# A recurrent sandwich block on one Trainium2 core: rounding GpSimd's weight pieces by two adding transfers instead of two elementwise instructions

## What is computed

```python
def layer_1(x, W_in, b_in, W_out, b_out, gamma, beta):
    u = einsum('bsd,hd->bsh', x, W_in) + b_in
    def step(state, u_t):
        s = tanh(u_t + state * gamma + beta)
        return (s, s)
    states = scan(step, 0, u)
    return einsum('bsh,dh->bsd', states, W_out) + b_out

def quantized_matmul(x, w, scale):
    wq = w.astype(float8_e4m3fn).astype(x.dtype)
    return einsum('bsi,io->bso', x, wq) * scale

def layer_2(x, gate_w, up_w, down_w, gate_scale, up_scale, down_scale):
    gate = silu(quantized_matmul(x, gate_w, gate_scale))
    up = quantized_matmul(x, up_w, up_scale)
    return quantized_matmul(gate * up, down_w, down_scale)

x = x + layernorm(layer_1(layernorm(x), ...))
x = x + layernorm(layer_2(layernorm(x), ...))
```

## Time and profile before

| | |
|---|---|
| runs (median of 3) | 603.26 us (601.48 to 605.08) |
| the profiled execution | 603.18 us, its span 601.4 us |
| TensorE busy (PE) | 557.9 us, 93% |
| VectorE busy (DVE) | 398.2 us, 66% |
| ScalarE busy (ACT) | 325.5 us, 54% |
| GpSimd busy (POOL) | 208.7 us, 35% |
| chain that ended last | DVE 35%, PE 32%, ACT 21%, issue 5%, DMA 4% |
| transfers | 27.47 MB, all issued by SyncE |

### The profile page before, as it was taken

The page is one execution under the profiler, slowest core; times in us unless marked ns, Lnnn a source line. Parts: engine busy times, 40 slices in busy tenths (PEclk is TensorE's granted clock), DMA queues, the critical chain, the costliest instruction groups (busy, mean ns, idle before and its releaser), DMA issues.

```text
span 601.4 us, 10100 instructions
## 1 busy us (share of the span) xinstructions
PE 557.9 (93%) x2984; PEld 467.4 (78%) x2984; DVE 398.2 (66%) x1638; ACT 325.5 (54%) x1496; POOL 208.7 (35%) x335
## 2 busy tenths in 40 slices
PE   4999798899899999999999999999999997988993
PEld 4766465789779887988788988988798786876992
DVE  3987967778686666766685758665666677655213
ACT  2765564655557554755466545755575555551330
POOL 1100214356637232534244314432233233521622
PEclk9999899899999999999999999999999998999998
DMA  8774114001012001010012001200010000200000
GB/s 267 212 243 143 53 44 150 1 19 36 1 36 71 1 1 36 14 58 2 1 36 71 1 1 36 71 2 1 1 41 32 1 1 2 71 1 1 37 0 35
DMA packets 16598, 27.47 MB, mean 46 GB/s; under 512 B 2336, under 2 KB 4512, under 8 KB 16544
## 3 DMA queue, kind: packets, MB, share of 16 engines
q1 hardware_dynamic: 16544, 26.84, 13.9%
HBM read 22.63 MB, written 4.19 MB: 45 GB/s over the span
## 4 chain that ended last, share of the span: by engine, by line
DVE 35%; PE 32%; ACT 21%; issue 5%; DMA 4%; POOL 1%; SPq 1%; POOLq 0%; DVEq 0%; ACTq 0%
DVE recur L934 17%; ACT pairs L1215 12%; PE gate_up L854 11%; PE wide L811 6%; DVE fused L1050 5%; PE wide L880 4%; ACT pairs L1202 4%; PE wide L789 4%; ACT gated L1238 3%; PE wide L765 3%; ACT fused_hi L1254 2%; PE wide L898 1%; DVE x_norm L1024 1%; DVE z L1062 1%; DVE y L974 1%
## 5 line engine op out<-in xcount | busy, mean ns | idle before, releaser
L934 DVE TENSOR_TENSOR_SCAN recur<-recur,pairs 128x32 f32<-128x32 f32 x1024 | 235.7, 230 | 139.8 <-ACT pairs L1215 139.5
L1215 ACT ACTIVATE pairs<-recur 128x16 f32<-128x16 f32 x1024 | 191.8, 187 | 211.3 <-DVE recur L934 206.6
L811 PE MATMUL wide<-w_out_sb,pairs 128*128 128x512 f32 x256 | 116.0, 607 | 10.0 <-ACT pairs L1215 9.8
L1325 POOL TENSOR_TENSOR fused_lo<-fused,fused_hi 128x256 fp32r<-128x256 f32 x96 | 72.0, 750 | 145.6 <-ACT fused_hi L1254 145.5
L811 PEld LDWEIGHTS wide<-w_out_sb,pairs 128*128 128x128 f32 x256 | 74.7, 298 | 44.4 <-ACT pairs L1215 9.5
L789 PE MATMUL wide<-x_norm_t,w_in_sb 128*128 128x256 f32 x448 | 102.7, 386 | 6.3 <-ACT x_norm_t L1170 3.2
L854 PE MATMUL gate_up<-x_hi,gate_q 128*128 128x256 f32 x384 | 103.3, 301 | 4.4 <-DVE x_lo L1035 4.4
L789 PEld LDWEIGHTS wide<-x_norm_t,w_in_sb 128*128 128x128 f32 x448 | 85.1, 193 | 21.8 <-ACT x_norm_t L1170 6.3
L854 PE MATMUL gate_up<-x_lo,up_q 128*128 128x256 f32 x384 | 97.3, 286 | 0.0
L854 PE MATMUL gate_up<-x_hi,up_q 128*128 128x256 f32 x384 | 96.9, 285 | 0.0
L854 PE MATMUL gate_up<-x_lo,gate_q 128*128 128x256 f32 x384 | 96.5, 284 | 0.0
(11 more groups left out here) (93 smaller groups left out, 563.7 us busy)
## 6 DMA issues: line engine op xcount, KB each, us to landing
x_in<-x SPq DMA_DIRECT2D x16, 256.0 KB, 3.2
x_res<-x SPq DMA_DIRECT2D x16, 256.0 KB, 3.3
out<-z SPq DMA_DIRECT2D x14, 256.0 KB, 3.6
w_in_sb<-w_in_t SPq DMA_DIRECT2D x4, 512.0 KB, 5.6
w_out_sb<-w_out_t SPq DMA_DIRECT2D x8, 256.0 KB, 5.1
raw_own<-gate_w SPq DMA_DIRECT2D x6, 256.0 KB, 5.9
raw_own<-up_w SPq DMA_DIRECT2D x6, 256.0 KB, 4.2
z<-down_w SPq DMA_DIRECT2D x6, 256.0 KB, 3.0
```

The lines of the kernel that those rows point to most:

```text
L811: ins = eng.matmul(wide[b][:, :], pairs_by_batch[:, state_slots(n, b), :, j, 0].rearrange("p s b -> p (s b)"), w_out_sb[:, j, :], start=(j ...
L934: eng.tensor_tensor_scan(preact.rearrange("p c k -> p (c k)"), factors.rearrange("p c k -> p (c k)"), pairs[:, (t - 1) % RING, :, :].rearr ...
L1215: eng.activation(pairs[:, t % RING, :, 0], preact[:, :, 1], ACT.Tanh).then_inc(s_state, 1)
L1325: eng.tensor_tensor(fused_lo[:, f, :], fused[:, f, :], fused_hi[:, f, :].bitcast(F32), ALU.subtract).then_inc(s_fused_lo, 1)
```

## The change

For each of GpSimd's ten pieces the two elementwise instructions are replaced by three: GpSimd writes the negated constants into the piece's place in `down_q` (counted by a new semaphore), issues a transfer that adds the constants to the raw piece where it lies, and, when that has landed and the negation is done, issues a second transfer that adds the raw piece to the negated constants in `down_q`. Every wait on `s_pool_taken` counts 16 for a piece now, since a transfer raises its semaphore by 16. One line is added further up, so lines from 565 on stand one later. The timetable's costs are not changed.

```diff
--- before.py
+++ after.py
@@ -562,6 +562,7 @@
         s_constant = sem("s_constant")
         s_rounded = sem("s_rounded")
         s_taken = sem("s_taken")
+        s_pool_negated = sem("s_pool_negated")
         s_pool_rounded = sem("s_pool_rounded")
         s_pool_taken = sem("s_pool_taken")
         s_guard_step = sem("s_guard_step")
@@ -673,7 +674,7 @@
                     if before is not None:
                         eng.wait_ge(s_peak, 2 * (before + 1))
                         if by_pool(before):
-                            eng.wait_ge(s_pool_taken, pool_pieces(before + 1))
+                            eng.wait_ge(s_pool_taken, 16 * pool_pieces(before + 1))
                         else:
                             eng.wait_ge(s_rounded, tensor_pieces(before + 1))
                     eng.dma_start(raw[r], pieces[i][0]).then_inc(s_raw_in[r], 16)
@@ -698,7 +699,7 @@
                 yield T * n + 40.0
                 if n == 1:
 
-                    eng.wait_ge(s_pool_taken, pool_pieces(EARLY))
+                    eng.wait_ge(s_pool_taken, 16 * pool_pieces(EARLY))
                     eng.wait_ge(s_rounded, tensor_pieces(EARLY))
                     eng.wait_ge(s_peak, 2 * EARLY)
                 if n >= 2:
@@ -840,7 +841,7 @@
                             eng.wait_ge(s_x1_lo, batch * (p + 1))
                         if p == 0 and i % 4 == 0:
                             eng.wait_ge(s_taken, 2 * tensor_pieces(8 * (i // 4 + 1)))
-                            eng.wait_ge(s_pool_taken, pool_pieces(8 * (i // 4 + 1)))
+                            eng.wait_ge(s_pool_taken, 16 * pool_pieces(8 * (i // 4 + 1)))
                         if i < batch and p < LAST - 1:
 
                             eng.wait_ge(s_x_norm_t, batch * (p + 2) + i + 1)
@@ -864,7 +865,7 @@
                         eng.wait_ge(s_fused_lo, KI * p + i + 1)
                         if p == 0:
                             if by_pool(GATE_UP_PIECES + i):
-                                eng.wait_ge(s_pool_taken, pool_pieces(GATE_UP_PIECES + i + 1))
+                                eng.wait_ge(s_pool_taken, 16 * pool_pieces(GATE_UP_PIECES + i + 1))
                             else:
                                 eng.wait_ge(s_taken, 2 * tensor_pieces(GATE_UP_PIECES + i + 1))
                             if i == KI - 1:
@@ -1130,7 +1131,7 @@
                 eng.tensor_scalar(guard[:, 2:3], guard[:, 1:2], HUGE, HUGE, ALU.mult, ALU.mult).then_inc(s_guard_step, 1)
                 yield at["guard", 3]
                 eng.wait_ge(s_guard_step, 3)
-                eng.wait_ge(s_pool_taken, pool_pieces(NP))
+                eng.wait_ge(s_pool_taken, 16 * pool_pieces(NP))
                 eng.scalar_tensor_tensor(out=poisoned, in0=guard[:, 2:3], scalar=0.0, in1=poisoned.bitcast(F32),
                                          op0=ALU.mult, op1=ALU.add).then_inc(s_guard_step, 1)
 
@@ -1332,11 +1333,13 @@
                     src, constant = raw[raw_of[i]], rounders[:, i % NR, :].bitcast(F32)
                     yield at["pool_add", i]
                     eng.wait_ge(s_constant, i + 1)
+                    eng.tensor_scalar(pieces[i][1], constant, -1.0, 0.0, ALU.mult, ALU.add).then_inc(s_pool_negated, 1)
                     eng.wait_ge(s_peak, 2 * (i + 1))
-                    eng.tensor_tensor(src, src, constant, ALU.add).then_inc(s_pool_rounded, 1)
+                    eng.dma_start(src, constant, accum_op=ALU.add).then_inc(s_pool_rounded, 16)
                     yield at["pool_take", i]
-                    eng.wait_ge(s_pool_rounded, pool_pieces(i + 1))
-                    eng.tensor_tensor(pieces[i][1], src, constant, ALU.subtract).then_inc(s_pool_taken, 1)
+                    eng.wait_ge(s_pool_negated, pool_pieces(i + 1))
+                    eng.wait_ge(s_pool_rounded, 16 * pool_pieces(i + 1))
+                    eng.dma_start(pieces[i][1], src, accum_op=ALU.add).then_inc(s_pool_taken, 16)
 
             strands = [prepare(), low_parts(), round_weights()]
             for b in range(batch):
```

## The result

The changed kernel takes 619.5 us (median of 4 runs, 618.01 to 621.14), the kernel before 602.37 us beside it (4 runs): ratio 1.028, 95% interval 1.023 to 1.033. The forecast was 616.8 us, with a range of 606 to 637. The span grew from 601.4 to 617.9 us, by 16.5.

A forecast was written before the change was run, and what follows sets the result against it. The recurrence on VectorE was taken to end last in the edited stretch, with TensorE nearly full behind it. Waits of 1.3 + 6.9 + 5.9 - 0.5 = 13.6 us on 603.18 us gave 616.8 us, range 606 to 637.

The forecast's parts named there:

- first place: Pieces 26 and 27: piece 32's reload lands late, so VectorE's maxima at 106.33 come 1.3 us late.
- Second place: Pieces 29 to 31: piece 35's reload makes VectorE's maxima at 140.98 6.9 us late; the y root's wait hides in it.
- Third place: Pieces 34 and 35: the last guard step on VectorE, at 171.10, waits for the last landing, 5.9 us late.
- The gain: VectorE's exponent mask at 120.23, lengthened by GpSimd's add, stands beside the shorter negation instead: minus 0.5 us.
- D and L: D: GpSimd's time to issue a transfer, taken as 1.0 us; L: start of issue to landing, taken as 3.7 us.
- S: 3L + D, the sum in which both transfer prices enter at all three places: 12.1 us.
- VectorE blocks the issue: Rival: each issue waits 0.43 us for a VectorE mask or constants instruction on the shared port; 620.7 us, chance 0.11.
- the projection's own wait would grow past 2.12 us: Sign: TensorE's wait before the output projection at 160.68 grows past its earlier 2.12 us.
- TensorE waits a little for low part 4: Second place: low part 4 is queued behind the y root, but TensorE waits less than VectorE is late.
- GpSimd's busy time would fall by 18 us: Sign: GpSimd's busy time falls by about 18 us while the kernel's time rises.
- Two bounds of its rivals: Not slower: S under 5.7, 602.1 to 602.7 us, chance 0.04; nearly hidden: L 2.0 to 2.2, 603.2 to 606.3, 0.11.
- general form: max(0, S - 10.8) + max(0, S - 5.2) + max(0, S - 6.2) - 0.5, as growth for any S.

The follow-up runs named there:

- e5: Changed kernel with the timetable told the transfers' times, so each second issue stands later with other work between and VectorE's readers are placed by landings: 602.0 us, ratio 1.0002.
- e3: Changed kernel with the maxima of pieces 31 to 35 left out: 614.9 us, ratio 1.020.
- e6: Changed kernel with the last guard step on VectorE six steps of the recurrence later: 617.5 us, ratio 1.025.
- e7: As e3, with the y root moved ahead of piece 31 on GpSimd: 616.3 us, ratio 1.022.
- e1: Changed kernel keeping each piece's first transfer, with an elementwise subtraction for the second and no negation: 613.4 us, ratio 1.018.
- e9: Changed kernel plus one adding transfer of 1 KB issued by GpSimd at 83.16 us: 617.5 us, ratio 1.025.
- e4: Changed kernel plus one adding transfer of 1 KB issued by GpSimd at 8.29 us: 617.9 us, ratio 1.027.
- e2: Changed kernel with an elementwise add for the first transfer, keeping negation and second transfer, whose landing is awaited piece by piece: 610.0 us, ratio 1.013.
- e10: Changed kernel with the loads of pieces 29 and 30 cut to 8 of 512 columns: 621.3 us, ratio 1.031.
- e11: As e5, with pieces 24 and 25 also GpSimd's, twelve pieces in place of ten: 605.1 us, ratio 1.006.
- e12: Changed kernel with the loads of x for the third block and of pieces 29 and 30 cut to 8 of 512 columns: 619.2 us, ratio 1.029.

## Why the prediction held

**The mechanism.** GpSimd in order behind landings, VectorE in order behind GpSimd: shown by e5, which has the same instructions, the same bytes and the same engines, with GpSimd's and VectorE's programs in another order, and none of the loss; and by the waits named in e3, e6 and e7. Forecast of the changed kernel, 616.8 us; measured, 619.5. Growth forecast 13.6 us; span's growth 16.5. By scans the terms miss by +1.6 us (first place), +1.3 (the constants of piece 32, not in the sum), -1.8 (second), -1.2 (third), -0.2 (gain) and +3.3 (what the sum lacked). That the total is nearer than that is partly luck, since the misses have both signs.

**D and L.** Taken as 1.0 and 3.7 us. Measured: issues of 1.09 and 0.87 us in the mean for the pieces in raw_own, landings of 3.6 and 3.2. At the second place piece 29's first issue starts at 134.01 and piece 30's second at 143.06, which lands 3.2 us later, at 146.3. Of these 12.3 us piece 30's negation takes 0.57 (138.38 to 138.95), so S is 11.7 us, against 12.1. The Trainium skill, DMA: Bandwidth & Descriptors ("Anatomy of one DMA"), led to an estimate of L = 2.6 us and 608.9 us for the kernel; these transfers landed in 3.2 to 3.6, so the rows of the trace were the better guide.

**First place: +1.3 forecast, +2.9 measured.** The failing step is one L for all transfers: piece 26's first one landed in 6.0 us, and piece 27 was taken at 106.3, not at 104.8. It also makes the reload of piece 31 late (1.87 us), which the prediction passed over for that of piece 32 (0.82 us).

**Second place: +6.9 forecast; +5.1, and +1.3 just before it at the constants of piece 32, measured.** The constants reuse piece 28's, so they wait for its second landing, 0.66 us: a wait on VectorE that I had not listed. The other half is that they take 0.94 us beside low part 2, in place of 0.42. Piece 35's reload lands when it does, so what VectorE lost here it doesn't lose again there. The sum, 6.4, is within 0.5 of the forecast by a term that the forecast did not have. That the root hides behind the reload was right (e3); that the residual hides behind the root I did not see (e7).

**Third place: +5.9 forecast, +4.7 measured.** Piece 35 landed 13.1 us behind the end of low part 11, not 13.7: the negation takes 0.57 us before the issue starts, not 0.8, twice. And low part 11 came 9.4 us late, when the recurrence was 9.8 late already.

**The gain: -0.5 forecast, -0.7 measured.**

**What the sum lacked: 1.4 us at 168.40 and 1.9 us after scan 278.** The first is a mask that started 0.13 us after an issue of GpSimd and lasted 1.80 us instead of 0.43. Behind that issue stood low part 10:

```profile
168.88 1.03 POOL L1326 TENSOR_TENSOR fused_lo<-fused,fused_hi 128x256 fp32r<-128x256 f32 x1
```

The mask ends at 170.20, 0.29 us after this low part. So it is with every mask or constants instruction over 0.5 us in the traces of all fourteen kernels (39 of them): it ends 0.28 to 0.30 us after an arithmetic instruction of GpSimd, as the mask of 120.23 in the kernel before does after the add. Where only an issue overlaps one, as at 120.99 and 121.46 in e1, at 123.98 in e9 and at 169.13 in e4, it takes 0.42 to 0.43. The rival "VectorE blocks the issue" thus had the sufferer wrong, and an issue alone is not shown to hold VectorE up; what part it has before a low part, no run isolates. SBUF — State Buffer of the Trainium skill ("A bandwidth-pool intuition that's wrong") warns of a transfer of GpSimd's stretched to 3.1 us by a VectorE copy that keeps it from writing descriptors. The longest issue here took 1.22 us. One in e5, at 135.72, overlaps a constants instruction and took 1.53, so these runs show nothing like 3.1, and at most a few tenths.

The second comes after the last of the three places. 1.2 of the 1.9 us are there by 208 us, and TensorE's clock is the likely cause of these: it was granted 0.89 of full from 190 to 206 us, where the kernel before had 1.00 over the same work (179 to 192); no run isolates that. The other 0.7 come at scan 959, at 523.57 us, far behind the change. e1, e2 and e3 lose 0.7 to 1.0 us at the same scan and e5, which loses nothing in the end, 0.5, so that part isn't traced to the change.

Earlier in the same trace the clock can be seen at work. TensorE's two waits just before the y projection, and the granted clock (third number from the end) in two stretches before and after:

```profile
165.68 0.47 PE L881 MATMUL wide<-down_q,fused_hi 128*128 128x512 f32 x1 [1.73 <-DMA down_q<-raw_own]
...
168.73 9.56 PE L812 MATMUL wide<-w_out_sb,pairs 128*128 128x512 f32 x16 [1.89 <-ACT pairs L1216]
```

```profile
160.00:169.00 9.00, 5.38 (x35) 4.49 (x34) 5.97 (x24) 5.32 (x25) 5.11 (x8) 0.88 0.48 87
169.00:179.00 10.00, 10.00 (x25) 5.57 (x25) 6.28 (x23) 3.70 (x19) 5.06 (x8) 0.77 0.37 66
```

The 16 matmuls of that projection take 9.56 us; in e5, at full clock, 7.24. In the changed kernel the guard's wait stands right behind and covers this; in e2, with no such wait, it cost VectorE the 1.94 us shown above.

**Its signs.** That the projection's own wait would grow past 2.12 us was wrong: it is 1.89, because TensorE arrives late too, having waited 2.52 us for low part 4 at 150.93 and 1.73 us for a landing at 165.68. "TensorE waits a little for low part 4" had that too small. That GpSimd's busy time would fall by 18 us was wrong, for a reason of bookkeeping: 208.0 us against 208.7. The issues of its transfers are counted as busy, ten first ones of 1.07 us in the mean and ten second ones of 0.87, 19.4 us, and the negations add 7.9; together 27.3 for the 25.7 removed, though their recorded spans overlap a little. GpSimd was not relieved at all, it was only made to stand between.

**Two bounds of its rivals.** By the prediction's own general form VectorE waits from S = 5.2 us on, not from 5.7, and with D at 1.0 an L of 2.0 to 2.2 us gives S of 7.0 to 7.6 and 605.3 to 606.5 us, not 603.2 to 606.3. Both belong to small chances and change nothing in the forecast.

## What to carry to other kernels

When an elementwise operation on an in-order engine is replaced by a transfer, ask first what that engine does between issue and landing: issue several before the first result is needed, and move every reader by the landing time; e5 against the changed kernel is 17 us for the two together. Behind one late instruction look for the next two on the same engine: taking away the first wait of a stack (e3, e6, e7) wins little or nothing. And a transfer issued by the engine itself is no relief to it if issue and preparation (0.9 to 1.1 us, twice, and 0.8) cost what the operation did.

## What was not expected of the hardware

- The clock of TensorE over the same 16 matmuls goes with what it did just before them. In the changed kernel it had stood 1.73 and 1.89 us shortly before, and the clock granted from 169 to 179 us was 0.77 of full (of the two levels, 1.2 and 2.4 GHz, it was at the lower for part of the stretch): the projection took 9.56 us. In e2 it had stood 4.01 us at a stretch: 0.70, 9.98 us. In the kernel before (2.12 us) and in e5 (2.02 us) it was at 1.00, 7.24 us. All fourteen kernels side with this. Where the last waits before the projection came to 0.1 to 2.3 us together (before, e5, e7, e10, e11), it took 7.24 us; where they came to 3.2 to 4.1 us (the others), 8.60 to 9.98. e10 has the changed kernel's wait right before the projection, 1.90 us, but 0.36 us in place of the 1.73: its row is the last below. So a wait of TensorE can cost more than its length.

```profile
164.00:174.00 10.00, 9.81 (x16) 5.01 (x17) 4.74 (x20) 3.58 (x19) 6.20 (x7) 0.70 0.16 29
```

```profile
161.00:170.00 9.00, 8.62 (x27) 6.24 (x28) 5.41 (x24) 4.06 (x22) 4.63 (x6) 1.00 0.54 98
```

```profile
168.27 7.24 PE L813 MATMUL wide<-w_out_sb,pairs 128*128 128x512 f32 x16 [1.90 <-ACT pairs L1217]
```

  The first is e2, the second e5, the third e10.
- Transfers that add, 256 KB within SBUF, issued by GpSimd, land in 3.2 to 3.6 us in the median, 0.3 to 0.7 us more than a 256 KB load; with several in flight, 5.5 us (e5).
- One and the same transfer (the first of piece 26) held GpSimd 5.3 to 6.8 us from its issue to the next in all eight kernels that issued it in this place with both transfers in order behind each other (e3, e4, e6 to e10 and e12), with many bytes or few in the loads beside it. Loads were in flight beside it every time.
- A mask of VectorE was held up beside an issue of GpSimd that a low part followed: 1.80 us at 168.40 here and 1.79 us at the same place in e3, where GpSimd's issue had begun 0.14 us earlier. Both end 0.29 us after the low part; beside an issue alone masks took 0.43 (e1, e4, e9).
